# Dealing VectorE's side steps out anew beside the tiles of a fused FFN, mixer, FFN kernel

## The reference, cut to what matters

```python
x = x + 0.5 * ffn(layernorm(x))
x = x + attn(layernorm(x))       # the mixer
x = x + 0.5 * ffn(layernorm(x))  # the same weights
```

## Time and profile before

| | us |
|---|---|
| Median of 3 runs | 683.49 (682.07 to 683.65) |
| Profiled execution | 683.5 |
| Its span, first to last instruction | 681.7 |
| TensorE busy | 648.2 |
| VectorE busy | 547.5 |
| GpSimd busy | 473.3 |
| ScalarE busy | 426.2 |

### The profile page before, as it was taken

The page is one execution under the profiler, slowest core; times in us unless marked ns, Lnnn a source line. Parts: engine busy times, 40 slices in busy tenths (PEclk is TensorE's granted clock), DMA queues, the critical chain, the costliest instruction groups (busy, mean ns, idle before and its releaser), DMA issues. The chain is left out here.

```text
span 681.7 us, 9627 instructions
## 1 busy us (share of the span) xinstructions
PE 648.2 (95%) x2813; PEld 504.8 (74%) x2813; DVE 547.5 (80%) x1587; ACT 426.2 (63%) x837; POOL 473.3 (69%) x467
## 2 busy tenths in 40 slices
PE   7899989999999999989999899999999999999997
PEld 6686767887776778767787677777787777767685
DVE  5888777988868889787987879787988977967765
ACT  3656666675576675767657675667577577555554
POOL 1256657775877967878687776888786677676564
PEclk9899999999999999999999999999999999999999
DMA  8102010000221212011211202012000010100101
GB/s 210 58 17 59 23 43 24 16 21 31 79 51 46 66 39 74 32 47 50 79 35 48 67 15 79 19 63 66 12 5 20 2 19 1 30 7 16 20 1 31
DMA packets 56917, 27.64 MB, mean 41 GB/s; under 512 B 21281, under 2 KB 52897, under 8 KB 56865
## 3 DMA queue, kind: packets, MB, share of 16 engines
q1 hardware_dynamic: 56144, 26.97, 13.8%
q10 hardware_dynamic: 720, 0.07, 0.1%
HBM read 17.91 MB, written 9.11 MB: 40 GB/s over the span
## 5 line engine op out<-in xcount | busy, mean ns | idle before, releaser
L700 POOL TENSOR_TENSOR hid_lo<-hid,hid_hi 128x512 fp32r<-128x512 f32 x270 | 349.1, 1296 | 174.8 <-ACT hid_hi L830 174.3
L1007 DVE TENSOR_TENSOR weighted<-gate_ps,wb 128x512 f32<-128x512 f32 x256 | 175.0, 684 | 93.4 <-ACT gate_ps L822 86.6
L830 ACT ACTIVATE hid_hi<-hid 128x512 fp32r<-128x512 f32 x272 | 170.6, 627 | 94.9 <-DVE hid L1020 94.0
L822 ACT ACTIVATE gate_ps<-gate_ps 128x512 f32<-128x512 f32 x256 | 148.5, 580 | 79.8 <-PE gate_ps L1344 78.6
L1020 DVE TENSOR_TENSOR hid<-weighted,up_ps 128x512 f32<-128x512 f32 x256 | 173.4, 677 | 6.8 <-issue 0.9
L1412 PE MATMUL down_ps<-hid_lo,wt_hi 128*128 128x512 f32 x272 | 108.1, 398 | 0.5 <-DVE hid_lo L1028 0.2
L1409 PE MATMUL down_ps<-hid_hi,wt_hi 128*128 128x512 f32 x272 | 107.9, 397 | 0.5 <-ACT ffn_sb L840 0.5
L1410 PE MATMUL down_ps<-hid_hi,wt_lo 128*128 128x512 f32 x272 | 107.5, 395 | 0.0
L1342 PE MATMUL up_ps<-xT_hi,wt_hi 128*128 128x512 f32 x170 | 70.5, 415 | 9.7 <-DVE hid L1020 9.4
L1342 PE MATMUL gate_ps<-xT_hi,wt_hi 128*128 128x512 f32 x170 | 70.4, 414 | 2.9 <-DVE weighted L1007 2.8
L1343 PE MATMUL up_ps<-xT_lo,wt_hi 128*128 128x512 f32 x170 | 67.4, 397 | 0.0
(11 more groups left out here) (218 smaller groups left out, 1068.4 us busy)
## 6 DMA issues: line engine op xcount, KB each, us to landing
x_hbm<-raw_gate SPq DMA_DIRECT2D x14, 256.0 KB, 2.0
raw_up<-x_hbm SPq DMA_DIRECT2D x56, 64.0 KB, 1.9
wb<-w_hbm SPq DMA_DIRECT2D x40, 64.0 KB, 2.2
x_ln<-in_L_attn_x SPq DMA_DIRECT2D x8, 256.0 KB, 3.0
x_res<-in_L_attn_x SPq DMA_DIRECT2D x8, 256.0 KB, 2.7
out_x<-x SPq DMA_DIRECT2D x7, 256.0 KB, 2.3
wb<-w_tiles_hbm SPq DMA_DIRECT2D x20, 64.0 KB, 2.4
ffn_hbm<-raw_gate SPq DMA_DIRECT2D x5, 256.0 KB, 2.0
```

Source lines behind the costliest of these rows:

```text
L700: nc.gpsimd.tensor_tensor(hid_lo[s][:, :], hid[s][:, :], hid_hi[s][:, :].bitcast(F32), ALU.subtract)\
L822: nc.scalar.activation(bank[:, :] if j else silu_sb[:, :], bank[:, :], ACT.Silu).then_inc(silu_done, 1)
L830: nc.scalar.activation(hid_hi[s][:, :], hid[s][:, :], ACT.Copy).then_inc(hid_hi_done, 1)
L1007: V.tensor_tensor(weighted[j % 2][:, :], gate_ps[n % BANKS][:, :], wb[u % 2][:, :], ALU.mult)\
```

## The change

All tables of slots are written anew. The steps, their instructions and their order within one chain stay; only the tiles and half tiles beside which they are issued differ. The 26 route steps, which were spaced evenly (`even(first, last)`), now have a slot each. Below the shared tables in full, and of the BEGIN and END tables what the text speaks of (eight leading blanks are taken off each line; most lists of route slots are left out):

```diff
--- before.py
+++ after.py
@@ -387,104 +387,120 @@
...
-ADD = {"copy ffn 1": 1, "shuffle ffn 1": 3, "sum ffn 1": 13, "next x_res": 14}
-PROJECT = {"stats 2": 0.5, "meanvar 2": 1.5, "norm 2": 2, "normalise 2": 6, "shuffle 2": 7.5, "xT high 2": 11,
-           "low 2": 11, "mixer gate": 13, "tanh gate": 13, "mixer value": 15, "copy value": 15,
-           "add ln_b": 15}
-NORM4 = {"normalise 3": 3, "scale 3": 4, "x2": 6, "stats 4": 8, "meanvar 4": 9, "norm 4": 9,
-         "normalise 4": 10, "shuffle 4": 11.5}
+ADD = {"copy ffn 1": 2, "shuffle ffn 1": 2.5, "sum ffn 1": 12, "next x_res": 16.5}
+PROJECT = {"stats 2": 0.5, "meanvar 2": 0.5, "norm 2": 1, "normalise 2": 6, "shuffle 2": 7, "xT high 2": 11,
+           "low 2": 11, "mixer gate": 14, "tanh gate": 14, "mixer value": 15, "copy value": 16,
+           "add ln_b": 16}
+NORM4 = {"normalise 3": 1, "scale 3": 2, "x2": 4, "stats 4": 6.5, "meanvar 4": 9, "norm 4": 9,
+         "normalise 4": 12, "shuffle 4": 12.5}
 PREPARE = {"xT high 1": 0, "low 1": 0, "router 1": 2, "spread logits 1": 2, "shuffle logits 1": 3.5,
-           "silu logits 1": 5, "route 1": even(4, 13.5), "weights 1": 14}
-BEGIN_NEXT = {"stats 1": 15, "meanvar 1": 16}
-MIXER = {"conv": (0, 0.5, 1.5, 2.5, 3, 5), "y high": 6, "y low": 6, "mixer out": 8, "shuffle mixer": 9.5,
-         "sum mixer": 13, "stats 3": 14.5, "meanvar 3": 16, "norm 3": 16}
-ROUTE4 = {"xT high 4": 0, "low 4": 0, "router 4": 2, "spread logits 4": 2, "shuffle logits 4": 3.5,
-          "silu logits 4": 5, "route 4": even(4, 13.5), "weights 4": 14}
-OUTPUT = {"copy ffn 4": 1, "transpose ffn 4": 5, "halve ffn": 7, "add ffn 4": 8, "store": 9}
-NEXT = {"norm 1": 1, "normalise 1": 4, "next x_ln": 5, "shuffle 1": 6}
+           "silu logits 1": 5,
+           "route 1": (4, 4.5, 5, 5, 5.5, 6, 6.5, 6.5, 8, 8, 9, 9, 9.5, 10, 10.5, 10.5, 11, 11.5, 12, 12,
+            12.5, 13, 13.5, 13.5, 14, 14), "weights 1": 14.5}
+BEGIN_NEXT = {"stats 1": 14, "meanvar 1": 14}
+MIXER = {"conv": (0, 0.5, 1.5, 2.5, 3, 4), "y high": 5, "y low": 6, "mixer out": 9, "shuffle mixer": 10.5,
+         "sum mixer": 13, "stats 3": 14.5, "meanvar 3": 16.5, "norm 3": 16}
+ROUTE4 = {"xT high 4": 0, "low 4": 0, "router 4": 2, "spread logits 4": 3, "shuffle logits 4": 3.5,
+          "silu logits 4": 5,
+          "route 4": (4, 4.5, 5, 5, 5.5, 6, 6.5, 6.5, 7, 7.5, 8, 8, 8.5, 9, 9.5, 9.5, 10, 10.5, 11, 11,
+           11.5, 12, 12.5, 12.5, 13, 13.5), "weights 4": 14.5}
+OUTPUT = {"copy ffn 4": 2, "transpose ffn 4": 4, "halve ffn": 6, "add ffn 4": 9, "store": 10}
+NEXT = {"norm 1": 1, "normalise 1": 4, "next x_ln": 2.5, "shuffle 1": 8}
 BEGIN = [
     [
-        ({"stats 1": 0.5, "meanvar 1": 0.5, "norm 1": 1, "normalise 1": 2, "next x_ln": 3, "transpose 1": 4,
-          "xT high 1": 4, "xT low 1": 4.5, "router 1": 5, "silu logits 1": 6, "route 1": even(6, 13.5),
-          "weights 1": 14}, 1),
-        ({"stats 1": 8, "meanvar 1": 9, "norm 1": 9, "normalise 1": 10, "next x_ln": 11.5,
-          "shuffle 1": 11.5}, 2),
+        ({"stats 1": 0, "meanvar 1": 1.5, "norm 1": 0, "normalise 1": 2, "next x_ln": 4.5, "transpose 1": 4,
+          "xT high 1": 4, "xT low 1": 4.5, "router 1": 5, "silu logits 1": 6,
...
+           12, 12.5, 12.5, 13, 13.5, 14), "weights 1": 15}, 1),
+        ({"stats 1": 5, "meanvar 1": 8, "norm 1": 8, "normalise 1": 10, "next x_ln": 9, "shuffle 1": 11.5}, 2),
     ],
     [
-        ({"copy ffn 1": 2, "transpose ffn 1": 3, "add ffn 1": 5.5, "next x_res": 7}, 0),
-        ({"stats 2": 5.5, "meanvar 2": 5.5, "norm 2": 6, "normalise 2": 7, "transpose 2": 10, "xT high 2": 10,
-          "xT low 2": 10, "mixer gate": 12, "tanh gate": 12, "mixer value": 14, "copy value": 14,
-          "add ln_b": 16}, 0),
-        ({"conv": (15, 15.5, 16.5, 16.5, None, None)}, 0),
-        ({"xT high 1": 0, "low 1": 0, "router 1": 2, "spread logits 1": 2, "shuffle logits 1": 3,
-          "silu logits 1": 4, "route 1": even(3, 13), "weights 1": 14}, 2),
-        ({"stats 1": 8, "meanvar 1": 8.5, "norm 1": 8, "normalise 1": 9, "next x_ln": 10.5,
-          "shuffle 1": 10.5}, 3),
+        ({"copy ffn 1": 2, "transpose ffn 1": 5, "add ffn 1": 5.5, "next x_res": 8.5}, 0),
+        ({"stats 2": 5.5, "meanvar 2": 5.5, "norm 2": 6, "normalise 2": 7, "transpose 2": 9,
+          "xT high 2": 10, "xT low 2": 10, "mixer gate": 11, "tanh gate": 13, "mixer value": 14,
+          "copy value": 14, "add ln_b": 15}, 0),
+        ({"conv": (14.5, 15, 15.5, 16, None, None)}, 0),
+        ({"xT high 1": 0, "low 1": 0, "router 1": 2, "spread logits 1": 2, "shuffle logits 1": 2.5,
+          "silu logits 1": 4,
...
+           11.5, 12, 12, 12.5, 13), "weights 1": 13.5}, 2),
+        ({"stats 1": 7, "meanvar 1": 7, "norm 1": 9, "normalise 1": 11, "next x_ln": 14.5,
+          "shuffle 1": 11.5}, 3),
     ],
     [
-        ({"conv": (None, None, None, None, 0, 0), "y high": 0, "y low": 1, "mixer out": 6, "mixer sum": 6.5,
-          "stats 3": 6.5}, 0),
-        ({"meanvar 3": 6.5, "norm 3": 7, "normalise 3": 8, "scale 3": 8, "x2": 9, "stats 4": 13,
...
+        ({"conv": (None, None, None, None, 0, 0.5), "y high": 1, "y low": 0, "mixer out": 6,
+          "mixer sum": 6.5, "stats 3": 6.5}, 0),
+        ({"meanvar 3": 6.5, "norm 3": 7, "normalise 3": 8, "scale 3": 8, "x2": 10, "stats 4": 12,
...
     [
-        ({"transpose 4": 0, "xT high 4": 0, "xT low 4": 0.5, "router 4": 2, "silu logits 4": 4,
-          "route 4": even(2.5, 12.5), "weights 4": 14}, 0),
-        ({"conv": (0, 0.5, 1, 2, 3, 4), "y high": 5, "y low": 5, "mixer out": 7, "shuffle mixer": 8.5,
-          "sum mixer": 12, "stats 3": 13, "meanvar 3": 14.5, "norm 3": 16}, 1),
-        ({"copy ffn 1": 1, "shuffle ffn 1": 3.5, "sum ffn 1": 6, "next x_res": 7}, 2),
-        ({"stats 1": 9, "meanvar 1": 10, "norm 1": 10, "normalise 1": 11, "next x_ln": 12,
-          "shuffle 1": 12}, 4),
+        ({"transpose 4": 0, "xT high 4": 0, "xT low 4": 1.5, "router 4": 2, "silu logits 4": 4,
...
+           10.5, 11, 11.5, 11.5, 11.5, 12.5), "weights 4": 13.5}, 0),
+        ({"conv": (0, 0.5, 1, 2, 3, 5), "y high": 5, "y low": 5, "mixer out": 8, "shuffle mixer": 8.5,
+          "sum mixer": 12, "stats 3": 15, "meanvar 3": 15, "norm 3": 15}, 1),
+        ({"copy ffn 1": 2, "shuffle ffn 1": 2, "sum ffn 1": 6, "next x_res": 9}, 2),
+        ({"stats 1": 6.5, "meanvar 1": 7, "norm 1": 9, "normalise 1": 12, "next x_ln": 9.5,
+          "shuffle 1": 12.5}, 4),
     ],
 ]
 END = [
     [
-        ({"conv": (0.5, 1, 1.5, 2.5, 3.5, 4.5), "y high": 5, "y low": 4, "mixer out": 7, "mixer sum": 7.5,
+        ({"conv": (0.5, 1, 1.5, 1.5, 3, 4), "y high": 5, "y low": 5, "mixer out": 7, "mixer sum": 7.5,
...
-        ({"xT high 4": 0, "low 4": 0, "router 4": 2, "spread logits 4": 2, "shuffle logits 4": 3,
-          "silu logits 4": 4, "route 4": even(3.5, 13.5), "weights 4": 14}, 4),
-        ({"copy ffn 4": 3, "transpose ffn 4": 4, "halve ffn": 6, "add ffn 4": 5, "store": 7}, 3),
...
+        ({"xT high 4": 1, "low 4": 0, "router 4": 2, "spread logits 4": 2, "shuffle logits 4": 2.5,
+          "silu logits 4": 4,
...
+           11.5, 12, 12.5, 12.5, 13, 13.5), "weights 4": 15.5}, 4),
+        ({"copy ffn 4": 2, "transpose ffn 4": 3, "halve ffn": 4, "add ffn 4": 7, "store": 6.5}, 3),
...
+          "add ln_b": 15}, 6),
     ],
     [
-        ({"conv": (0, 0, 0.5, 0.5, 2.5, 3.5), "y high": 5, "y low": 5, "mixer out": 7, "mixer sum": 8,
-          "stats 3": 8.5}, 6),
...
+        ({"conv": (0, 0, 0.5, 0.5, 2.5, 4.5), "y high": 5, "y low": 5, "mixer out": 7, "mixer sum": 7.5,
+          "stats 3": 9}, 6),
...
-          "shuffle logits 4": 2, "silu logits 4": 3, "route 4": even(2.5, 12.5), "weights 4": 14}, 5),
-        ({"copy ffn 1": 3, "transpose ffn 1": 4, "add ffn 1": 6.5}, 7),
+          "shuffle logits 4": 2, "silu logits 4": 3,
...
+           10.5, 11, 11.5, 11.5, 12, 12.5), "weights 4": 13}, 5),
+        ({"copy ffn 1": 2, "transpose ffn 1": 3, "add ffn 1": 5.5}, 7),
     ],
     [
-        ({"transpose 4": 0, "xT high 4": 0, "xT low 4": 1.5, "router 4": 3, "spread logits 4": 3,
-          "shuffle logits 4": 3.5, "silu logits 4": 4, "route 4": even(3.5, 13), "weights 4": 14}, 6),
-        ({"copy ffn 4": 2, "transpose ffn 4": 5, "halve ffn": 5, "add ffn 4": 9, "store": 11}, 4),
-        ({"stats 2": 0.5, "meanvar 2": 2, "norm 2": 0, "normalise 2": 2, "transpose 2": 9, "xT high 2": 9,
+        ({"transpose 4": 0, "xT high 4": 0, "xT low 4": 1, "router 4": 3, "spread logits 4": 3,
+          "shuffle logits 4": 2.5, "silu logits 4": 4,
...
+           11, 11, 11.5, 12, 12, 12.5, 13), "weights 4": 13.5}, 6),
+        ({"copy ffn 4": 2, "transpose ffn 4": 5, "halve ffn": 7, "add ffn 4": 12, "store": 9.5}, 4),
...
-          "add ln_b": 12}, 7),
-        ({"conv": (13, 13.5, 14, 14.5, 15, 15.5), "y high": 16, "y low": 16}, 7),
+          "add ln_b": 11}, 7),
+        ({"conv": (12.5, 12.5, 14, 14.5, 15, 15.5), "y high": 16, "y low": 16}, 7),
     ],
```

(10 more changed lines are left out.)

30 lines of the change are left out of this document (18 added, 12 removed), and 5 rows, old and new, of tables (BEGIN, END).

## The result

The kernel after takes 652.5 us (median of four runs, 651.7 to 653.4) against 682.8 before (four runs, 681.5 to 683.7): a ratio of 0.956, with a 95% interval of 0.953 to 0.958. A later repeat, five runs against nine, gave 653.1 against 683.3, or 0.955 (0.954 to 0.957). The gain is 30.3 us. The forecast was 662.0, a gain of 21.4, and 652.5 lies half a microsecond under the low end of the range of 653 to 674: the forecast was too cautious. Of the cases listed it is the rival "all returns with no new wait", 653.6 us, that came about.

The account below looks back on a forecast made before the run. TensorE was taken to be bound by waits for late VectorE steps (two banks, strict order), 29.9 us at most. Terms -12.0 - 4.4 - 9.0 + 4.0 = -21.4 from 683.5 gave 662 us, range 653 to 674.

Parts of the forecast that it names:

- all returns with no new wait: Rival for the whole kernel: the full 29.9 us of waits comes back, 653.6 us; chance 0.07.
- What it may add: Five places in (1,3), (4,5) twice, (4,6) and (1,1) look worse; 0.8 us each, +4.0 us in sum.
- the outer units: Term for (1,0) to (1,3), (1,7), (4,4) and (4,6): smaller waits return -9.0 us, between 0 and -14.
- The shared units: Two terms: (4,0) to (4,3) return -12.0 us, (1,4) to (1,6) return -4.4 us.
- the prediction's signs: If right: (4,1) lasts 38.0 to 38.5 us, (1,5) 37.6 to 38, TensorE's hid and weigh waits under 8.
- GpSimd's bunched steps: In (4,0) to (4,3), x2 comes earlier; hid_lo 4 ends at 15.4 us, needed at 17.3, so it stays hidden.
- The five orders: Places in (1,3), (4,5) twice, (4,6) and (1,1), each said to cost 0 to 1.5 us, taken as 0.8.
- (1,0)'s term: In (1,0), tile 8's VectorE steps fall from 1.72 to 0.87 us, returning -1.2 us.
- cause (c): In (4,0) to (4,3), ScalarE's normalise 4 waits 1.39 us for GpSimd's norm 4, holding silu; VectorE idles 2.36.
- nearly all: Four waits in (4,1) are worth 3.1 us and one in (1,5) 1.5, nearly all that these units lose.
- upper bound of 29.9: Whole kernel: 34 gate and up waits, 20.7 us shown plus 0.27 each, 29.9 us at most returnable.
- 1.2 us to spare: At shared units' ends: weights shuffled later still let "weigh" 1 meet gate 3 at 6.3 us; cost nothing.

Follow-up runs that it names:

- e4: The kernel after, with the five places that the prediction priced at +0.8 us each mended: 653.5 us (0.957 of before).
- e10: The kernel after, with the next block's first norm in (1,0) and (1,3) put back to its old places: 656.0 us (0.961 of before).
- e8: The kernel after, with the seven shared units' routing weights shuffled at 16 instead of 14.5: 661.2 us (0.968 of before).
- e11: The kernel after, with the seven shared units' routing weights shuffled at 15.5 instead of 14.5: 654.5 us (0.957 of before).
- e1: The kernel before, with only the five tables of the shared second-FFN units taken from the change: 671.2 us (0.982 of before).
- e5: The kernel after, with copy ffn 1 in tile 1, its shuffle at 3, normalise 3 and scale 3 in tile 3 in (4,0) to (4,3): 657.8 us (0.963).

## Why the prediction was wrong, and where it was right

The time came out below the range. The mechanism held, and terms of the sum were mis-sized: first of all "What it may add", +4.0, where the runs showed nothing added, then the outer units, -9.0, which returned 11.6.

**Right: the bound and the mechanism.** TensorE lost its time by VectorE's lateness in strict order over two banks, and dealing the steps out returned it. The shared units came within 0.3 us each of their terms and ended at the floor: -12.9 for -12.0 and -5.2 for -4.4. Of the prediction's signs, the two kinds of unit came out just under the lengths that it gave (37.80 for 38.0 to 38.5, 37.53 for 37.6 to 38), and the waits far under 8 us. The Trainium skill ("Perfetto Trace Analysis", optimization strategy) says that gaps that repeat can mean too little SBUF or PSUM for the next tile; that was not the case here: the banks are the same two, and the gaps are gone.

**Right: what was costed at nothing, in the shared units.** GpSimd's bunched steps stayed hidden. In (4,1) of the kernel after hid_lo 4 is the first of the two here, so it ends some 16.0 us after the unit's start at 256.31 (15.4 counted), and down 4 asks for it at 17.3, as counted:

```profile
270.98 2.63 POOL L716 TENSOR_TENSOR hid_lo<-hid,hid_hi 128x512 fp32r<-128x512 f32 x2
```

```profile
273.58 0.40 PE L1428 MATMUL down_ps<-hid_lo,wt_hi 128*128 128x512 f32 x1
```

The cover is 1.3 us, not 1.9. The mixer's data in tile 13 of (1,5) were there when GpSimd came, without the 0.8 us of wait that I had counted. The weights at 14.5 cost nothing.

**Wrong: "What it may add", +4.0.** This is the largest miss, and the step that failed. The five orders cost 0.1 us or less each, as far as the runs can tell (e4). I had priced each at half of the one wait of 1.51 in (1,5), although I had myself put the tolerance at over 2 us and had seen light tiles behind each of the five; the runs say that a lateness that stays inside the cushion costs nothing, not half.

**Wrong in size: the outer units, -9.0.** They returned 11.6. (1,0)'s term, -1.2 for an overfull tile, was mis-sized because cause (c) was passed over there (e10: 1.6 for it and 0.4 for the tile); (1,3)'s -1.0 measured -2.3; (1,7) and (4,4), -1.0, measured -2.0, by waits at side and down products that the count of 34 did not contain. On the other side (4,6), -1.9, returned only 0.9: two of its four waits went, as counted, but two others came, at gate 4 (0.40, behind the copy that was left in tile 1) and at down 5 (0.16, for hid_lo). And (1,1), -2.6, returned 2.0.

**Wrong in size: taking "nearly all", 3.0 of 3.1,** in the shared units: they returned 3.24 and 1.73, which is 1.7 us over seven units.

4.0 + 2.6 + 1.7 make 8.3 of the 9.5 us between forecast and median. Of the last 1.2 the base is 0.7 (I took the profiled 683.5, the median here is 682.8), and the rest lies within the scatter of the set-up. That the gain lands on the upper bound of 29.9 is luck: the gate and up waits that went are worth 18.6 + 28 x 0.27 = 26.2 us, and the rest of the units' 29.8 came from waits at side and down products and from lateness too short to be shown, which the bound didn't count. So 29.9 was not the most that the change could return.

**Wrong, but without effect: the weights' "1.2 us to spare".** The count was for the wrong product (e8, e11): a shuffle one tile later costs 1.4 us over seven units, one that is 1.5 tiles later 7.6 instead of 15.

## What to carry to other kernels

When an engine's work is dealt out beside a stream of tiles, keep an account (none was drawn up here for a whole unit) of its lateness from tile to tile (what it must do, less the room of a tile, never below the lead that the buffers allow) and price an order only where that account runs over; an order that makes it wait inside the cushion costs nothing, and a wait's place in the trace says where the account ran over, not which step filled it. Look in every stage for a consumer placed one tile behind a producer on another engine, here a normalise behind GpSimd's norm: ScalarE stood 1.0 us in (1,0) and 1.4 in each of (4,0) to (4,3), with a silu behind it. And where steps are moved later, follow the last of them through its round trip to its reader: the better dealt unit lost 2.5 of its 2.9 us again in the next one.

## What the runs showed that I had not expected

The lengths of the seven shared units but (4,0) repeat to 0.03 us over all profiles in which their tables and those of the unit ahead are the same, so a single profile tells a change of 0.1 us in one such unit, where the median of a whole kernel, scattered over 2 us, can't. The scatter comes from the start. Busy time by stretch of the first 20 us and of unit (1,0), in the kernel before, then in e1, which has the same tables there:

```profile
0.00:20.00 20.00, 15.70 (x82) 13.52 (x82) 11.77 (x43) 8.03 (x16) 2.02 (x11) 1.00 0.83 224
20.00:65.96 45.96, 41.68 (x187) 31.63 (x186) 38.30 (x126) 26.31 (x51) 22.38 (x23) 0.96 0.09 27
```

```profile
0.00:21.93 21.93, 17.66 (x81) 15.25 (x82) 13.44 (x57) 8.24 (x16) 2.02 (x11) 1.00 0.79 208
21.93:65.89 43.96, 40.51 (x187) 30.48 (x186) 36.73 (x114) 26.15 (x51) 22.46 (x23) 1.00 0.09 26
```

The unit starts 1.9 us later in e1 and is 2.0 shorter. In the kernel before TensorE stands 2.7 us at the unit's start for the first routing weights, and from 24 to 28 us its granted clock is 0.60 (2.4 GHz is 1.00, 1.2 GHz is 0.50); in e1 the clock is 1.00 throughout. The end of (1,0) is what can be compared: 64.2 to 66.0 us with the tables of before (three profiles, mean 65.3), 61.6 to 63.6 with those of after (twelve, mean 62.6). That is 2.7 us for (1,0) and the set-up together. Where the clock was 1.00 in (1,0), it lasted 43.6 and 44.0 us against 41.0 to 41.9 (eleven profiles, mean 41.4), from which I take the 2.4 of the table. The profile of e5 starts as the one of before does, with a stand of 2.7 us and a mean clock of 0.96 in the unit, and its (1,0) lasts 43.45 us against 45.96, 2.5 less. Why the start differs from run to run stays open, as does why (4,0) alone is up to 0.5 us longer than its like in several of the profiles.
